# Attention and a mixture of experts on one core: a unit's side job is issued ahead of pv instead of between its last score matmuls

## The reference

```
x = x + layernorm(attention(layernorm(x)))      # 16 heads of 16 values, with biases
x = x + layernorm(experts(layernorm(x)))        # 16 experts, 8 chosen per token, and a shared one

attention: q = (x Wq' + bq) / 4, k = x Wk' + bk, v = x Wv' + bv, by head
           softmax(q k') v, then Wo' and its bias
```

## Time and profile before

| | |
|---|---|
| profiled execution | 2944.34 us |
| its span, first to last instruction | 2942.6 us |
| attention stage | about 0 to 1650 us, its steady part from 150 us on |
| PE busy | 2772.4 us, 94% of the span |
| DVE busy | 2241.8 us, 76% |
| ACT busy | 1635.6 us, 56% |
| reductions of the maxima, L611 | 2048 of 681 ns |
| exponentials, L539 | 2048 of 600 ns |

### The profile page before, as it was taken

One profiled execution on the slowest core, in us unless ns is written; L12 is line 12 of the kernel. 1 busy time (PEld: TensorE's weight loads), 2 busy tenths in 40 slices (PEclk: granted clock), 3 DMA queues, 4 the chain that ended last, 5 costly groups with the idle time before them and its releaser, 6 DMA issues. The chain is left out here.

```text
span 2942.6 us, 47567 instructions
## 1 busy us (share of the span) xinstructions
PE 2772.4 (94%) x16514; PEld 1689.3 (57%) x16514; DVE 2241.8 (76%) x4691; ACT 1635.6 (56%) x3095; POOL 916.9 (31%) x976
## 2 busy tenths in 40 slices
PE   5999999999999999999999459999999999999997
PEld 3433343343334433433333248888888888888886
DVE  4898999999999999999898156666666666666654
ACT  1477777777777777777777333333333333333332
POOL 4041453533634535336334510111111111111112
PEclk8899999999999999999999679999999999999999
DMA  5213333233134332331331143222322232223222
GB/s 91 48 27 54 63 75 61 60 62 62 44 60 64 78 57 59 63 64 34 55 63 33 31 119 102 80 80 80 79 78 80 80 78 78 80 80 79 78 73 54
DMA packets 136783, 197.39 MB, mean 67 GB/s; under 512 B 22352, under 2 KB 84960, under 8 KB 134496
## 3 DMA queue, kind: packets, MB, share of 16 engines
q1 hardware_dynamic: 136544, 194.36, 30.4%
HBM read 108.81 MB, written 17.30 MB: 43 GB/s over the span
## 5 line engine op out<-in xcount | busy, mean ns | idle before, releaser
L611 DVE TENSOR_REDUCE score_max<-sm_bank 128x1 f32<-128x512 f32 x2048 | 1301.5, 681 | 119.9 <-PE sm_bank L354 116.2
L539 ACT ACTIVATE probs<-st_bank 128x512 f32<-128x512 f32 x2048 | 1088.7, 600 | 337.7 <-PE st_bank L342 336.0
L354 PE MATMUL sm_bank<-qk_stack 64*128 64x512 f32 x2048 | 804.1, 465 | 18.6 <-DMA qk_stack<-qk_stack 10.9
L342 PE MATMUL st_bank<-qk_stack 64*128 64x512 f32 x2048 | 761.6, 453 | 37.9 <-ACT probs L539 31.3
L354 PEld LDWEIGHTS sm_bank<-qk_stack 64*128 64x128 f32 x2048 | 332.6, 187 | 579.6 <-DVE score_max L611 535.4
L364 PE MATMUL o_bank<-probs,v_quad 128*32 128x512 f32 x4096 | 547.1, 606 | 8.4 <-ACT o_sb L519 7.3
L1326 DVE TENSOR_TENSOR gated<-gate_act,u_bank 128x512 f32<-128x512 f32 x256 | 175.9, 687 | 311.5 <-ACT gate_act L1157 311.5
L1157 ACT ACTIVATE gate_act<-g_bank 128x512 f32<-128x512 f32 x272 | 162.5, 597 | 428.2 <-PE u_bank L1063 428.0
L342 PEld LDWEIGHTS st_bank<-qk_stack 64*128 64x128 f32 x2048 | 316.7, 184 | 119.3 <-ACT probs L539 91.7
L1168 ACT ACTIVATE h_hi<-h 128x512 fp32r<-128x512 f32 x272 | 172.0, 632 | 318.7 <-DVE h L1329 284.1
L1077 PE MATMUL y_bank<-f_w_hi,h_hi 128*128 128x256 f32 x1088 | 311.9, 287 | 5.7 <-DVE h_lo L1337 5.6
(11 more groups left out here) (190 smaller groups left out, 3830.2 us busy)
## 6 DMA issues: line engine op xcount, KB each, us to landing
cb<-comb_dram SPq DMA_DIRECT2D x256, 256.0 KB, 3.7
qk_stack<-qk_parts SPq DMA_DIRECT2D x360, 128.0 KB
x_in<-in_x SPq DMA_DIRECT2D x8, 1024.0 KB, 7.2
o_part<-o_sb SPq DMA_DIRECT2D x256, 32.0 KB, 1.9
sum_part<-o_sb SPq DMA_DIRECT2D x256, 32.0 KB, 2.0
x_res<-in_x SPq DMA_DIRECT2D x16, 512.0 KB, 4.0
x<-x_res SPq DMA_DIRECT2D x16, 512.0 KB, 3.1
f_x_in<-x SPq DMA_DIRECT2D x16, 512.0 KB, 3.9
```

Of the source, the lines that this page charges most:

```text
L342: mm(st_bank[tile % RING][:, :], k_stack[q][p][rows, kc * CH:(kc + 1) * CH], q_stack[q][p][rows, f * HALF:(f + 1) * HALF], start=True, sto ...
L354: mm(sm_bank[n % RING][:, :], q_stack[q][p][rows, tok:tok + CH], k_stack[q][p][rows, half * HALF:(half + 1) * HALF], start=True, stop=True ...
L539: nc.scalar.activation(probs[kc % 2][:, j, :], st_bank[(4 * U + j) % RING][:, :], ACT.Exp).then_inc(exp_done, 1)
L611: v.reduce_max(score_max[f][:, HC * (2 * p + e) + c, half:half + 1], sm_bank[n % RING][:, :], AX_X).then_inc(smax_read, 1)
```

## The change

The five lines that issue the job of a unit move up, from behind `scores(3)` to ahead of `pv`. Each unit's order on TensorE was scores(0), scores(1), maximum(0,0), pv, maximum(0,1), scores(2), maximum(1,0), scores(3), job, maximum(1,1). It becomes scores(0), scores(1), maximum(0,0), job, pv, maximum(0,1), scores(2), maximum(1,0), scores(3), maximum(1,1). The lists of the other engines are the same.

```
                     scores(0)
                     scores(1)
                     maximum(0, 0)
+                    if u in JOBS and not skipped(JOBS[u], first, last):
+                        kind, off, i, part = JOBS[u]
+                        job(kind, b + off, i, part)
                     pv(U, S, s, kc)
                     maximum(0, 1)
                     scores(2)
                     maximum(1, 0)
                     scores(3)
-                    if u in JOBS and not skipped(JOBS[u], first, last):
-                        kind, off, i, part = JOBS[u]
-                        job(kind, b + off, i, part)
                     maximum(1, 1)
```

## The result

The changed kernel takes 3262.6 us (median of four runs, 3250.17 to 3271.45) against 2944.71: 318 us more, ratio 1.108, 95% interval 1.1037 to 1.1122. The direction and most of the size were forecast (3184), but the time lies 2.6 us above the range (3115 to 3260). The main terms of the sum, the free unit and the late bank, hold almost to the hundredth of a microsecond; what the sum left out is the clock, rival B.

A forecast was written before the change was run, and what follows sets the result against it. ScalarE and VectorE were taken to set the free unit's loop, while TensorE never idles in QK units. Lost cover and late bank reads summed to 34.5 us a batch, 241 over seven, some 240 net: 3184 us, range 3115 to 3260.

The forecast's parts named there:

- the free unit: Unit without a job: the loop pv, scores(2), two exponentials, pv takes 2.70 us, TensorE idling in it; stays 2.70.
- the late bank: Job straight behind another waits for job_bank's read: QK 1.79 us more, 2.21 with BN stats, V and OP 0.87.
- rival B: TensorE's clock also falls at each of 11 VectorE waits a batch: 119 us on top, 3303 us; 14%.
- the lost cover: Job ahead of pv no longer fills the last pair's wait: matmul job unit 3.60 us, not 3.22, 0.38 more.
- Weights of pv loading under the job: Between job and pv, possible overlap: unit 3.43 instead of 3.60 us, 52 us less, 3132 us; 3.60 was taken.
- the XT of unit 23: Attention stage, XT jobs 23 and 27: unit 3.30 us against 3.13, 0.3 us a batch in the sum.
- Rival A: Only the job's cover goes, the bank is never late: 13.6 us a batch, 95 in all, 3039 us; 10%.
- C: One change of shape less, 0.17 us a job unit, if scores(1)'s pair starts at once: 43 less, 2901 us; 3%.
- D: VectorE or DMA, not TensorE's order, sets the pace and nothing moves: 2944 us; 2%.

The follow-up runs named there:

- experiment 3: The changed kernel with both ScalarE's and VectorE's reads of a job also moved about 1.7 us earlier: 3043.7 us, ratio 1.0345.
- Experiment 4: The changed kernel with ScalarE's read of a job alone moved ahead, VectorE's subtraction left in place: 3237.69 us, ratio 1.0997.
- the one with four matmuls: The changed kernel with 4 extra full-array matmuls ahead of each of the 11 jobs a batch that wait for VectorE's read: 3183.8 us, ratio 1.0819.

## Why the prediction was wrong, by its own steps

**The loop of the free unit and the lost cover: right.** 3.60 forecast, 3.60 measured, and 101.5 us in experiment 3 where the cover alone is lost (95 by the sum).

**Weights of pv loading under the job: settled.** No gain; 0.90 measured against bounds of 0.72 and 0.89, so the lower figure of 3132 us had no ground.

**The bank: right.** The job behind a QK with statistics starts at T+4.52 for a forecast T+4.54 and behind OP the unit takes 4.10 for 4.09. Experiment 4 tells the two readers apart and experiment 3 removes the wait. All moved terms together, with the clock held up, make 3183.8 us; the sum said 3184. So close a figure is partly luck: small errors are in it on both sides. The unit that ends with the OP job of unit 5 took 3.96 and not 3.60, since VectorE's split and seed in units 3 and 4 delay the maximum ahead of it, and the one that ends with the XT of unit 23 rose from 2.73 to 3.46, where the sum had 0.17 more. (Rival A's terms add up to 13.4 a batch and 94 us, not 13.6 and 95.)

**The clock: this is the step that failed.** The sum had nothing for it, and rival B had 14%, "since the new stretches have more work between the idle times than the one that fell". The row in hand was a fall behind 2.58 us idle and none behind 0.65; I took the new idle times of 1.4 to 1.9 us, which lie between, for nearer to the harmless end, and the work between them for a protection. It did not protect here: the clock fell again and again behind them, 79 us in all, two thirds of the 119 that B had at its worst. The price was right, 87.3 us for 60 stretches or 1.46 each in the profiled runs, for a forecast 1.55; only not all of the 77 waits paid it. The mechanism, its place and its price were on record; the chance was wrong, and with it the middle. With half of B's 119 in the sum the forecast would have been 3243, with the time 20 us from it.

The trace of the kernel before has one more row, which I had not read:

```profile
1120.73 0.26 PEld L342 LDWEIGHTS st_bank<-qk_stack 64*128 64x128 f32 x2 [1.63 <-DMA qk_stack<-shift_row]
...
1117.00:1127.00 10.00, 8.72 (x58) 3.88 (x58) 8.75 (x20) 7.12 (x15) 0.00 (x0) 1.00 0.06 14
```

Here the loads were idle for 1.63 us, as long as in the shorter of the new waits (1.51 to 2.06), and the granted clock stayed at 1.00. It would have spoken for my choice, and wrongly: this stretch stands alone, while the new ones come up to five within 35 us. One idle stretch at full clock is no evidence for a row of them. The Trainium skill, "TensorE: Matmul & The Clock Gate", section "HAM oscillation — how this bites in real kernels", tells of a matmul kernel that fell to the lower clock at every tile behind a wait for a transfer and paid the fall each time. The traces agree, with waits for the read of a bank in the transfer's place and shorter than that kernel's; that a wait which comes back many times a batch is paid for many times was the part of the rule to weigh.

**Rivals A, C, D:** A fell as the whole answer but is what experiment 3 shows when the bank is early. C fell: in the unit of 1188.83 the pair with scores(1) still waits for an exponential and goes at T+2.21, so nothing of the move brought it forward. D fell with the 318 us.

## What to carry to other kernels

Before moving a step in an in-order list, ask what it covers where it stands and whether the readers of its buffer answer in time where it goes; here both were read off a few units of the timeline to a few hundredths of a microsecond. When a change opens idle stretches on TensorE again and again, put a price on the clock into the sum itself, not into a rival, unless a row shows idle stretches as long, and as often, at full clock. Where such a wait can't be removed, harmless matmuls in it can be worth more than they cost, as they were here.

## What the runs showed of the hardware that was not expected

- Idle stretches of TensorE of 1.5 to 2.1 us in the weight loads (1.0 to 1.8 between matmuls), 11 in a batch of 242 us, brought TensorE's granted clock down to its lower level for parts of the attention stage (0.91 over 400 us); a single one of 1.63 us in the kernel before left it at 1.00. Two extra matmuls in each were almost enough to hold it (0.974 against 0.976), one was not (0.961).
- A us at the lower level cost 0.39 us here by the changed kernel against the one with four matmuls; by that price two more comparisons came out within 1 us.
- 308 matmuls more made the kernel 79 us faster.
